# A gated cross-attention and FFN block: TensorE's turn through the attention in another order

## The reference, cut to what matters

```python
def xattn(query, key, value, mask, Wq, bq, Wk, bk, Wv, bv, Wo, bo):
    q, k, v = heads(query @ Wq.T + bq), heads(key @ Wk.T + bk), heads(value @ Wv.T + bv)
    scores = einsum('bhqd,bhkd->bhqk', q, k) / sqrt(HD)
    scores = where(mask[:, None], finfo.min, scores)
    attn = softmax(scores, axis=-1)
    ctx = einsum('bhqk,bhkd->bhqd', attn, v)
    return merge(ctx) @ Wo.T + bo

def ffn(x, Wg, bg, Wt, bt, W1, b1, W2, b2):
    gate = softmax(x @ Wg + bg); thr = sigmoid(x @ Wt + bt) * 0.125
    w = maximum(gate - thr, 0); w = w / where(sum(w) == 0, 1, sum(w))
    h = gelu(einsum('td,edf->etf', x, W1) + b1)
    return einsum('te,etd->td', w, einsum('etf,efd->etd', h, W2) + b2)

x = x + tanh(g_xattn) * xattn(layernorm(x), ctx, ctx, mask, ...)
x = x + tanh(g_ffn) * ffn(layernorm(x), ...)
```

## Time and profile before

| | us |
|---|---|
| median of 3 runs (lowest, highest) | 622.63 (621.52, 625.18) |
| the profiled execution, its span | 622.45, 620.6 |
| first phase, start of turn 3 to start of turn 14 | 66.48 to 218.27 |
| TensorE busy over the span | 588.7 (95%) |
| VectorE, ScalarE, GpSimdE busy | 484.4, 378.5, 176.3 |

### The profile page before, as it was taken

How to read it: one execution, slowest core, us unless ns; L and a number is a source line. 1 busy time by engine, 2 the same in 40 slices (tenths; PEclk the granted TensorE clock), 3 DMA queues, 4 the chain that set the end, 5 groups by cost and what they waited for, 6 DMA issues and landing times.

```text
span 620.6 us, 13748 instructions
## 1 busy us (share of the span) xinstructions
PE 588.7 (95%) x4482; PEld 448.7 (72%) x4482; DVE 484.4 (78%) x941; ACT 378.5 (61%) x625; POOL 176.3 (28%) x223
## 2 busy tenths in 40 slices
PE   6689899999999998999999999999999999999998
PEld 5455566666666655788878788787887887887886
DVE  6367677777777776588788889888888888888886
ACT  2144455555555554867776767676777676776773
POOL 5443444444453221112203212212112112122121
PEclk9799899999999999999999999999999999999999
DMA  5865554556555420051111221121121121121210
GB/s 142 244 172 157 162 161 141 142 155 170 161 152 158 142 55 5 6 103 51 43 60 35 64 60 52 51 66 40 46 68 51 37 64 51 51 64 38 68 51 17
DMA packets 43998, 55.12 MB, mean 89 GB/s; under 512 B 9520, under 2 KB 27824, under 8 KB 42416
## 3 DMA queue, kind: packets, MB, share of 16 engines
q1 hardware_dynamic: 43504, 53.99, 31.0%
q10 hardware_dynamic: 448, 0.53, 0.3%
HBM read 39.16 MB, written 14.81 MB: 87 GB/s over the span
## 4 chain that ended last, share of the span: by engine, by line
PE 78%; DMA 4%; ACT 4%; DVE 2%; SPq 2%; issue 2%; ACTq 0%; DVEq 0%
PE ps_h L1033 10%; PE ps_h L1035 9%; PE ps_h L1034 9%; PE ps_y L1048 9%; PE ps_y L1050 9%; PE ps_y L1049 9%; DMA kq_st<-maxT 4%; PE misc L1011 4%; PE scores L949 3%; PE scores L977 3%; PE scores L989 2%; PE scores L966 2%; ACT probs L541 1%; PE misc L1088 1%; PE misc L1180 1%
## 5 line engine op out<-in xcount | busy, mean ns | idle before, releaser
L565 ACT ACTIVATE h_sb<-ps_h,b_sb 128x512 f32<-128x512 f32 x256 | 175.9, 689 | 102.3 <-PE ps_h L1035 92.2
L709 DVE TENSOR_TENSOR h_low<-h_sb,h_high 128x512 fp32r<-128x512 f32 x256 | 164.6, 683 | 0.1
L504 POOL TENSOR_TENSOR yT<-yT,weighted 128x512 f32<-128x512 f32 x54 | 70.9, 1313 | 277.8 <-DVE weighted L891 277.8
L705 DVE CAST h_high<-h_sb 128x512 fp32r<-128x512 f32 x128 | 97.9, 765 | 52.6 <-ACT h_sb L565 52.4
L686 DVE TENSOR_REDUCE neg_max<-scores 128x8 f32<-128x1024 f32 x64 | 77.9, 1222 | 42.3 <-PE scores L949 42.3
L1033 PE MATMUL ps_h<-x_high,w_high 128*128 (+1 forms) x256 | 101.8, 398 | 2.1 <-ACT h_sb L565 2.0
L1048 PE MATMUL ps_y<-h_high,w_high 128*128 128x512 f32 x256 | 100.2, 391 | 0.3 <-ACT h_high L569 0.3
L1035 PE MATMUL ps_h<-x_high,w_low 128*128 (+1 forms) x256 | 99.8, 390 | 0.0
L1034 PE MATMUL ps_h<-x_low,w_high 128*128 (+1 forms) x256 | 99.7, 390 | 0.0
L1050 PE MATMUL ps_y<-h_high,w_low 128*128 128x512 f32 x256 | 99.7, 389 | 0.0
L1049 PE MATMUL ps_y<-h_low,w_high 128*128 128x512 f32 x256 | 99.6, 389 | 0.0
(11 more groups left out here) (127 smaller groups left out, 716.0 us busy)
## 6 DMA issues: line engine op xcount, KB each, us to landing
w_row<-w_scratch SPq DMA_DIRECT2D x64, 256.0 KB, 3.1
kq_st<-kq_scratch SPq DMA_DIRECT2D x64, 192.0 KB
kq_scratch<-kq_parts SPq DMA_DIRECT2D x30, 256.0 KB, 3.5
w_raw<-in_w_ffn SPq DMA_DIRECT2D x16, 256.0 KB, 3.3
kq_scratch<-kq_parts SPq DMA_DIRECT2D x32, 128.0 KB, 3.5
ctx_sb<-in_ctx SPq DMA_DIRECT2D x16, 128.0 KB, 2.7
out_y<-y_out SPq DMA_DIRECT2D x7, 256.0 KB, 2.3
x_all<-in_x SPq DMA_DIRECT2D x13, 128.0 KB, 2.2
```

The lines of the kernel that those rows point to most:

```text
L504: nc.gpsimd.tensor_tensor(yT[:], yT[:], weighted[:, e % 2, :], ALU.add).then_inc(added, 1)
L565: nc.scalar.activation(h_sb[:, j % HBUF, :], ps_h[:, j % 4, :], ACT.Gelu_apprx_tanh, bias=b1_sb[:, j:j + 1]).then_inc(h_done, 1)
L705: nc.vector.tensor_copy(h_high[:, j % HBUF, :], h_sb[:, j % HBUF, :]).then_inc(high_odd, 1)
L709: nc.vector.tensor_tensor(h_low[:, j % HBUF, :], h_sb[:, j % HBUF, :], h_high[:, j % HBUF, :].bitcast(F32), ALU.subtract).then_inc(low2_do ...
```

## The change

In `body` of TensorE's program three things move. `natural_rest(g, 0, u)` comes directly behind `natural(g, 0, u)`, ahead of the jobs `merged` and `x2T`. The turn of batch 0's maxima (`max0`) comes ahead of `transposed(g-1, 1, u)`, which then stands together with `transposed_rest(g-1, 1, u)`. `natural_rest(g, 1, u)` comes directly behind `natural(g, 1, u)`, ahead of `values(g-1, 1, u)`. The programs of the other engines are the same.

```diff
@@ -1061,6 +1061,7 @@
                     natural(g, 0, u)
+                    natural_rest(g, 0, u)
                 if (g := group_at(it, -2)) is not None:
...
@@ -1073,9 +1074,6 @@
                         second(0, 3)
-                if (g := group_at(it, 0)) is not None:
-                    u = g % 2
-                    natural_rest(g, 0, u)
                 if (g := group_at(it, -2)) is not None:
...
@@ -1110,9 +1108,6 @@
                     ins.then_inc(misc_full[bank_of("kq")], 1)
-                if (g := group_at(it, -1)) is not None:
-                    u = g % 2
-                    transposed(g, 1, u)
                 if (g := group_at(it, 0)) is not None:
                     if g == 0:
                         idle_turns(2)
...
@@ -1121,6 +1116,7 @@
                 if (g := group_at(it, -1)) is not None:
                     u = g % 2
+                    transposed(g, 1, u)
                     transposed_rest(g, 1, u)
...
@@ -1133,15 +1129,13 @@
                     natural(g, 1, u)
+                    natural_rest(g, 1, u)
                 if (g := group_at(it, -1)) is not None:
                     u = g % 2
                     values(g, 1, u)
                     if g == NG - 1:
                         first(0, 2)
                         first(0, 3)
-                if (g := group_at(it, 0)) is not None:
-                    u = g % 2
-                    natural_rest(g, 1, u)
```

## The result

The changed kernel takes 635.93 us (median of 4 runs) where the kernel before took 623.48 beside it: 1.020 times as long, interval 1.014 to 1.026. The forecast was 631.1 in a range of 624 to 637. The profiled executions are 635.55 and 622.45 us, their spans 633.7 and 620.6: 13.1 us apart.

What follows compares the result with a forecast made beforehand. PE was taken as nearly, not wholly, the bound, so new waits cost time at once. Full turns +6.4, turn 14 +1.2, turn 15 +0.75, turns 1 and 2 +0.3: 8.65 on 622.45 gives 631.1 us, range 624 to 637.

Steps and rivals of the forecast that it cites:

- Step 1: Batch 0's natural masks together: wo at 2.43 instead of 1.99, PE idling some 0.5; maxima ready at 5.32, not 4.88.
- Step 2: Batch 0's maxima turned before batch 1's transposed scores: new 0.43 idle, those scores at 5.49, against 4.51.
- Step 3: Batch 1's natural masks together before values: values at 9.35 against 8.31, v at 11.02 against 9.98, about 0.65 idle.
- Step 4: Turn's end: batch 0's transposed scores at 11.81 against 10.77, tail 2.57, turn 14.38 against 13.80; +6.4 us over eleven.
- the other tail: Turn's end taking 2.89 us instead of 2.57: full turn 14.70, +9.9 over eleven turns, whole 634.6.
- Step 5: Edge turns: turns 1 and 2 +0.3 us, turn 14 +1.2, turn 15 +0.75; turn 0 the same.
- (a): Rival, attention turns: PE is full and waits only trade places; 622.4 us, give or take 3; chance 0.13.
- (b): Rival, batch 0's maxima: their turn comes sooner, the DMA behind it is hidden; faster, 617.4 us; chance 0.07.
- (c): Rival, turns 14, 15 and perhaps 1: new waits make PE's clock fall, up to 1.7 us each; 636.2 us; chance 0.10.

Runs made afterwards that it cites:

- The first move alone: Kernel before with only batch 0's second pair of natural masks moved directly behind the first, ahead of merged: 627.22 us median, 1.005 times the kernel before.
- DVE's order: Changed kernel with, on DVE, the second half of batch 0's maxima ahead of the update of x_all: 629.67 us, 1.009 times the kernel before.
- turn 1 with the wait filled: Changed kernel with three idle matmuls ahead of the turn of batch 0's maxima in turn 1 alone: 640.24 us, one execution.
- the move on SyncE: Kernel before with two of four next-group kq_st loads issued behind the DMA of batch 0's maxima: 619.45 us (0.989); on another chip 618.73 (0.992).
- the third move alone: Kernel before with only batch 1's second pair of natural masks moved ahead of values: 627.47 us median, 1.003 times the kernel before.

## Why the prediction was right, point by point

**Step 1** (wo 0.44 late, maxima ready at 5.32). `wo` stands at 187.55, 2.42; L698 ends at 190.45, 5.32. To the hundredth. The first move alone and DVE's order show both halves of it.

**Step 2** (maxima's turn at 5.38 behind a new wait, transposed scores 5.49, exp 6.73, natural scores 7.87). The turn stands at 5.38. The scores follow it by 0.21, not 0.11: the 0.11 was read between this turn and a mask, and now sixteen score matmuls stand there. Exp comes 1.25 behind (1.24 taken), natural scores 1.17 behind that (1.14). So 8.01 instead of 7.87.

**Step 3** (values 9.35, v 11.02). Natural scores to values take 1.56, where I had 1.48 from two pairs of masks: 9.57. From values to `v` 1.68 (1.67 taken): 11.25. The wait on V1's copy is 0.59 (0.65).

**Step 4** (transposed scores of batch 0 at 11.81, tail 2.57, turn 14.38). They stand at 12.03, and the tail is 2.66, near the one taken. The turn is 14.69 here, 14.65 in the mean. This is the term that was mis-sized: +6.4 for eleven turns, measured +9.35. Four links were short by 0.10, 0.03, 0.08 and 0.09, 0.3 in a turn and some 3 in eleven. The range's upper end for this term, +9.9, came from the other tail, which did not occur; that it covers the measured value is luck in part.

**Step 5** (turns 1 and 2 +0.3, turn 14 +1.2, turn 15 +0.75). Measured: turn 1 +2.25, turn 2 -1.05, turn 14 +1.54, and +1.0 from turn 15's start to the FFN. Turn 1 lost the clock, which I had only as a rival; turn 2, which before had lost it behind its wait for the DMA, kept it. The sum is +3.7 where +2.25 was predicted. Most of the difference stands in turns 1 and 2, whose +0.3 was taken without a row; they came to +1.2. Compared by executions that kept the clock (turn 1 with the wait filled, 14.16 against 13.06; turn 2 14.36 against 13.52 with the move on SyncE) they lose +1.9, so the falls that changed places hid a part of what this term missed.

**The rivals.** (a) falls: PE at 95% was no reason for order not to matter, and PE's idle time in the full turns grew by 11.8 us. Of the three waits that (a) lets fall away the largest didn't: PE waits for ACT's exp before the natural scores 4.1 us in these turns, 3.7 before. (b) falls where the prediction put it, in DVE's queue, and what would have been won, had the maxima been first there, is shown by the run with DVE's order: not enough. (c) came true in part: the clock fell in turn 1 in all three profiles that have the changed order on PE and its wait there (1.52 to 1.54 us), and in turn 14 or 15 in some executions and not in others. The fall in turn 1 cost about 1.15 us there, where (c) had up to 1.7. It does not explain the full turns, where the clock was at 1.00.

## What to carry to other kernels

Ask of an instruction that stands oddly between two others what it covers: here two masks filled the time in which another engine copied what the next matmul needed, and bringing like things together opened that gap. Bringing a step forward did nothing here, because its input's producer, on another engine, had a job ahead of it in its own order that waited for this engine; the two orders must change together, and even then the waits that are opened elsewhere can cost more than is won (14.14 against 13.67 a turn). To size such a change, chain one turn from start to start, and take each link from a place where the same two instructions stand next to each other.

## What the runs showed of the hardware that was not expected

The clock fell to 0.50 behind rather short waits, and not always. It fell behind a single wait of 1.54 us in turn 1, behind one of 1.51 in turn 2 of the kernel before, behind 0.59 and 1.00 close together, and behind 1.17 and 0.77 close together in one execution (17.1 us at half rate, turn 14 at 19.70) but not in another (14.87). With DVE's order it fell in a full turn too, behind 0.59 and 0.46 (turn 11, 16.26). It kept to 1.00 behind 1.64 and 1.53 in turn 1 of two kernels, and behind 1.33 after turn 15 of the kernel with the move on SyncE. What decides it is open.

The falls go with a part of the difference between runs of one kernel: with the third move alone, the run with the highest mean clock (0.992) took 621.75 us and those at 0.973 took 630.70 and 630.83. With the wait in turn 2 taken away by the move on SyncE the runs lie closer together as well: 617.82 to 620.32 in ten, where the kernel before had 620.38 to 628.16 in fifteen beside them.
